# A state-space layer written out, its modulation columns read in place, and a residual of all items formed by GpSimd ahead of it

## The reference

```python
# layer 0: attention, then a stack of six local-attention and feed-forward blocks
x = x + ga * attn0(layernorm(x) * (1 + ca) + sa)
x = x + gb * ffn0(layernorm(x) * (1 + cb) + sb)      # this sum is "x3" below
# layer 1, with its own six vectors
h = layernorm(x) * (1 + ca) + sa
x = x + ga * state_space(h)                          # this sum is "x4"
h = layernorm(x) * (1 + cb) + sb
x = x + gb * (h @ (W + lilora).T + b)                # this sum is "x5", the output
```

## Time and profile before

| | |
|---|---|
| median of 3 runs | 4745.26 us (4742.04 to 4746.15) |
| the profiled execution | 4740.36 us |
| its span in the trace | 4738.6 us |
| granted TensorE clock, mean | 0.957 |
| `phase_c` | from about 4015.8 us to the end |
| from the first scan of item 6 to that of item 7 | 40.97 us |

### The profile page before, as it was taken

The page is one execution under the profiler, slowest core; times in us unless marked ns, Lnnn a source line. Parts: engine busy times, 40 slices in busy tenths (PEclk is TensorE's granted clock), DMA queues, the critical chain, the costliest instruction groups (busy, mean ns, idle before and its releaser), DMA issues. The chain is left out here.

```text
span 4738.6 us, 123474 instructions
## 1 busy us (share of the span) xinstructions
PE 4256.0 (90%) x45166; PEld 3182.7 (67%) x45166; DVE 4026.9 (85%) x7275; ACT 3756.6 (79%) x11543; POOL 3543.5 (75%) x2504
## 2 busy tenths in 40 slices
PE   6998699999999999999999999999999997688887
PEld 3555477777777777777777777777777775445453
DVE  4776798989989989889889899899998895598887
ACT  2555588888888888888888888888888886777774
POOL 0010699999999889999999999999899994444544
PEclk9999799999999999999999999999999998788888
DMA  1000111112111111111111112111111111000000
GB/s 26 7 6 2 47 51 38 45 42 55 52 40 45 45 52 51 40 44 45 52 47 44 43 47 54 45 44 41 49 51 41 45 39 31 0 4 3 3 3 5
DMA packets 118563, 168.62 MB, mean 36 GB/s; under 512 B 26563, under 2 KB 44422, under 8 KB 118022
## 3 DMA queue, kind: packets, MB, share of 16 engines
q1 hardware_dynamic: 109246, 160.92, 12.8%
q10 hardware_dynamic: 8776, 0.45, 0.1%
HBM read 20.79 MB, written 2.10 MB: 5 GB/s over the span
## 5 line engine op out<-in xcount | busy, mean ns | idle before, releaser
L1371 POOL TENSOR_TENSOR b_w<-b_w,b_vt 128x512 f32<-128x512 f32 x768 | 1174.5, 1539 | 256.1 <-DVE b_vt L1285 158.5
L1375 POOL TENSOR_TENSOR b_rn<-b_ssm,all_neg_half 128x16 f32<-128x16 f32 x384 | 1177.4, 3066 | 32.0
L1182 ACT ACTIVATE b_Pr<-ps,b_nm 128x96 f32<-128x96 f32 x3072 | 1000.5, 353 | 0.6
L1182 ACT ACTIVATION_READ_ACCUMULATOR b_Pr<-ps,b_nm 128x1 f32 x3072 | 677.1, 220 | 0.0
L1225 ACT ACTIVATE b_PT<-ps 96x512 f32<-96x512 f32 x768 | 456.3, 594 | 234.8 <-PE ps L1035 222.0
L1334 DVE TENSOR_TENSOR b_Pr<-b_Pr,b_rinv 128x384 f32<-128x384 f32 x768 | 614.2, 800 | 26.3
L1069 PE MATMUL ps<-b_Whi,b_xlo 128*128 128x512 f32 x1152 | 585.4, 508 | 32.9 <-DVE b_vt L1285 18.1
L998 PE MATMUL ps<-all_ident,b_w 128*128 128x128 f32 x3072 | 478.5, 288 | 141.5 <-ACT b_qkT L1153 99.9
L1283 DVE TENSOR_TENSOR b_w<-ps,until_b_rotab 128x512 f32<-128x512 f32 x768 | 523.7, 682 | 60.3 <-ACT b_sq L1202 57.3
L1153 ACT ACTIVATE b_qkT<-ps 128x512 f32<-128x512 f32 x768 | 460.6, 612 | 84.7 <-PE ps L998 83.4
L1285 DVE TENSOR_TENSOR b_vt<-ps,until_b_rotab 128x512 f32<-128x512 f32 x768 | 521.8, 679 | 0.0
(11 more groups left out here) (256 smaller groups left out, 9348.6 us busy)
## 6 DMA issues: line engine op xcount, KB each, us to landing
b_V<-b_Vraw SPq DMA_DIRECT2D x384, 192.0 KB, 2.6
b_V<-b_Vraw SPq DMA_DIRECT2D x384, 128.0 KB, 2.4
b_V<-b_Vraw SPq DMA_DIRECT2D x192, 64.0 KB, 2.2
b_Wraw<-in_L_ffn_Wqkv SPq DMA_DIRECT2D x36, 256.0 KB, 3.3
b_Wo<-in_L_ffn_Wo SPq DMA_DIRECT2D x6, 512.0 KB, 4.1
a_xtok<-in_L_attn_hidden_states SPq DMA_DIRECT2D x16, 128.0 KB, 2.1
out<-c_xout SPq DMA_DIRECT2D x16, 128.0 KB, 1.8
b_W<-in_L_ffn_W SPq DMA_DIRECT2D x6, 341.0 KB, 3.6
```

What stands on the lines that cost most here:

```text
L1182: last = nc.scalar.activation(s.Pr[:, r % 2, j, i], ps[:, S_BANK[j], i * KEYS:(i + 1) * KEYS], ACT.Exp, bias=s.nm[:, r, j, i:i + 1], accum ...
L1371: nc.gpsimd.tensor_tensor(rows, rows, s.vt[:, i % 4], ALU.add).then_inc(s.pool_add, 1)
L1375: nc.gpsimd.tensor_tensor(s.rn[:, j], s.ssm[:, j], g.neg_half[:, 0:HB], ALU.pow).then_inc(s.pool_r, 1)
```

## The change

`phase_c` is written out in full: no loop, so every item number is a constant. With constants the modulation columns are read in place from `all_mod`, and the three small tiles, their copies and the semaphores for them go. x3 is no longer made item by item on DVE and copied back by POOL. POOL makes it for all 16 items ahead of its first step, in place in `all_xT`: a multiplication by the gate (a column broadcast over 256), a wait, and an addition of `all_x2T`. PE transposes item m from `all_xT` as soon as that item is ready, and DVE waits once for all 16 before the first x4.

```diff
-DVE_X3, DVE_XD, DVE_Y, DVE_STATS1, DVE_X4, DVE_DELTA, DVE_STATS2, DVE_X5 = 3, 3, 5, 6, 7, 5, 8, 13
+DVE_XD, DVE_Y, DVE_STATS1, DVE_X4, DVE_DELTA, DVE_STATS2, DVE_X5 = 3, 5, 6, 7, 5, 8, 13
-POOL_X3, POOL_STATS1, POOL_STATS2 = 12, 1, 12
+POOL_STATS1, POOL_STATS2 = 1, 12
 def phase_c_steps(engine, body):
-    def whole(n):
+    for n in range(-2, NB + 2):
         body(StepC(n, n % 2, *[0 <= n + d < NB for d in (2, 1, 0, -1, -2)]))
-    for n in range(-2, 2):
-        whole(n)
-    with engine.Fori(1, NB // 2 - 1) as pair:
-        for odd in range(2):
-            body(StepC(2 * pair + odd, odd, True, True, True, True, True))
-    for n in range(NB - 2, NB + 2):
-        whole(n)
...
 # DVE
-                if step.inner:
-                    m_seq, m_at = known(m), known(m * NT)
                 if step.tail:
-                    t_at, gate = known(t * NT), known(t & 3)
-                    wait(dve, s.x5_ready, t)
-                    copy_mod(s.md_tail, 1, known(t), 2, 6).then_inc(s.md_tail_ready, 1)
+                    gates, x_tail = g.mod[:, 1, t], g.xT[:, t * NT:(t + 1) * NT]
...
                     if step.tail and slot == DVE_X4:
+                        if t == 0:
+                            dve.wait_ge(s.x3_ready, NB)
                         dve.wait_ge(s.op_full, t + 1)
...
-                    if step.inner and slot == DVE_X3:
-                        wait(dve, s.hT_ready, m)
-                        copy_mod(s.md_inner, 1, m_seq, 0, 2)
-                        copy_mod(s.md_x3, 0, m_seq, 5, 6).then_inc(s.md_ready, 1)
-                        wait(dve, s.x3_kept, m)
-                        dve.wait_ge(s.md_ready, m + 1)
-                        nc.vector.scalar_tensor_tensor(out=s.x3T[:], in0=g.xT[:, bass.ds(m_at, NT)], scalar=s.md_x3[:], in1=g.x2T[:, bass.ds(m_at, NT)],
-                                                       op0=ALU.mult, op1=ALU.add).then_inc(s.x3_ready, 1)
...
 # POOL
-                    if step.inner and slot == POOL_X3:
-                        pool.wait_ge(s.x3_ready, m + 1)
-                        nc.gpsimd.tensor_copy(g.xT[:, bass.ds(m_at, NT)], s.x3T[:]).then_inc(s.x3_kept, 1)
...
+            for m in range(NB):
+                x_item, gate = g.xT[:, m * NT:(m + 1) * NT], g.mod[:, 0, m, 5:6].broadcast_to((P, NT))
+                nc.gpsimd.tensor_tensor(x_item, x_item, gate, ALU.mult).then_inc(s.x3_scaled, 1)
+                pool.wait_ge(s.x3_scaled, m + 1)
+                nc.gpsimd.tensor_tensor(x_item, x_item, g.x2T[:, m * NT:(m + 1) * NT], ALU.add).then_inc(s.x3_ready, 1)
             phase_c_steps(pool, body)
...
 # ACT (hT2 the same with columns 3 and 4 of item t, and without its wait for md_tail_ready)
-                        act.wait_ge(s.md_ready, m + 1)
                         act.wait_ge(s.h_full, m + 1)
-                        nc.scalar.activation(s.hT[:], ps[:, F_BANK, NT:2 * NT], ACT.Identity, bias=s.md_inner[:, 0:1], scale=s.md_inner[:, 1:2]).then_inc(s.hT_ready, 1)
+                        nc.scalar.activation(s.hT[:], ps[:, F_BANK, NT:2 * NT], ACT.Identity, bias=g.mod[:, 1, m, 0:1], scale=g.mod[:, 1, m, 1:2]).then_inc(s.hT_ready, 1)
...
 # PE
-                        transpose_tokens(F_BANK, by_tile(s.x3T)).then_inc(s.x3_full, 1)
+                        transpose_tokens(F_BANK, by_tile(g.xT[:, m * NT:(m + 1) * NT])).then_inc(s.x3_full, 1)
```

More of the change, by code:

```diff
@@ L1436, in phase_c @@
         s.conv_diag = s.sb("conv_diag", [P, CC, TAPS, P]); s.D_diag = s.sb("D_diag", [P, CC, P])
-        s.md_x3 = s.sb("md_x3", [P, 1]); s.md_inner = s.sb("md_inner", [P, 2]); s.md_tail = s.sb("md_tail", [P, 4])
-        s.x3T = s.sb("x3T", [P, NT]); s.x3tok = s.sb("x3tok", [P, TT, P]); s.hT = s.sb("hT", [P, NT]); s.hT2 = s.sb("hT2", [P, NT])
+        s.x3tok = s.sb("x3tok", [P, TT, P]); s.hT = s.sb("hT", [P, NT]); s.hT2 = s.sb("hT2", [P, NT])
         s.xp = s.sb("xp", [P, CC, TAPS - 1 + NT]); s.h = s.sb("h", [P, 2, CC, NT]); s.sr = s.sb("sr", [P, 4, CC, NT])
@@ L1444, in phase_c @@
         s.l1 = LayerNormC(s, "l1"); s.l2 = LayerNormC(s, "l2")
-        s.w_in, s.zeroed, s.built, s.md_ready, s.x3_ready, s.x3_kept, s.x3_full, s.x3tok_ready, s.h_full, s.hT_ready = s.sems(
-            "w_in zeroed built md_ready x3_ready x3_kept x3_full x3tok_ready h_full hT_ready")
+        s.w_in, s.zeroed, s.built, s.x3_scaled, s.x3_ready, s.x3_full, s.x3tok_ready, s.h_full, s.hT_ready = s.sems(
+            "w_in zeroed built x3_scaled x3_ready x3_full x3tok_ready h_full hT_ready")
         s.in_full, s.xp_ready, s.conv_full, s.gate_ready, s.h_ready, s.xd_full, s.rounded, s.xd_ready, s.dl_full = s.sems(
@@ L1452, in phase_c @@
             "bu_dve yc_dve pool_mult rows_ready scan_done y_full y_ready op_full")
-        s.md_tail_ready, s.x4_ready, s.x4_full, s.x4tok_ready, s.h2_full, s.hT2_ready, s.lin_full, s.tmp_ready, s.x5_ready = s.sems(
-            "md_tail_ready x4_ready x4_full x4tok_ready h2_full hT2_ready lin_full tmp_ready x5_ready")
+        s.x4_ready, s.x4_full, s.x4tok_ready, s.h2_full, s.hT2_ready, s.lin_full, s.tmp_ready, s.x5_ready = s.sems(
+            "x4_ready x4_full x4tok_ready h2_full hT2_ready lin_full tmp_ready x5_ready")
         s.out_full, s.xout_ready, s.stored = s.sems("out_full xout_ready stored")
@@ L1531, in body @@
                         nc.vector.tensor_tensor(s.y[:], ps[:, Y_BANK].rearrange("p (c t) -> p c t", c=CC),
[L1532 removed]
+                                                s.sr[:, t % 4], ALU.mult).then_inc(s.y_ready, 1)
                     if step.tail and slot == DVE_X4:
+                        if t == 0:
+                            dve.wait_ge(s.x3_ready, NB)
                         dve.wait_ge(s.op_full, t + 1)
[L1535 removed]
+                        nc.vector.scalar_tensor_tensor(out=s.x4T[:], in0=ps[:, TAIL_BANK, 0:NT], scalar=gates[:, 2:3], in1=x_tail,
                                                        op0=ALU.mult, op1=ALU.add).then_inc(s.x4_ready, 1)
[L1537 to L1544 removed]
                     if step.tail and slot == DVE_STATS2:
@@ L1549, in body @@
                         dve.wait_ge(s.tmp_ready, t + 1)
-                        nc.vector.scalar_tensor_tensor(out=s.x5T[:], in0=s.tmp[:], scalar=s.md_tail[:, 3:4], in1=s.x4T[:], op0=ALU.mult, op1=ALU.add).then_inc(s.x5_ready, 1)
+                        nc.vector.scalar_tensor_tensor(out=s.x5T[:], in0=s.tmp[:], scalar=gates[:, 5:6], in1=s.x4T[:], op0=ALU.mult, op1=ALU.add).then_inc(s.x5_ready, 1)
                     if step.delta and slot == DVE_XD:
@@ L1581, in body @@
                 own = step.odd
-                if step.inner:
-                    m_at = m * NT if isinstance(m, int) else pool.snap(m * NT)
                 for slot in range(SLOTS):
@@ L1614, in body @@
                 own, other = step.odd, 1 - step.odd
-                if step.inner:
-                    gate = m & 3 if isinstance(m, int) else act.snap(m & 3)
                 for slot in range(SLOTS):
@@ L1672, in body @@
                         last.then_inc(s.h_ready, 1)
-                        nc.scalar.activation(s.sr[:, bass.ds(gate, 1)].rearrange("p a c t -> p (a c) t"), ps[:, F_BANK].rearrange("p (c t) -> p c t", c=CC),
+                        nc.scalar.activation(s.sr[:, m % 4], ps[:, F_BANK].rearrange("p (c t) -> p c t", c=CC),
                                              ACT.Silu).then_inc(s.gate_ready, 1)
@@ L1681, in body @@
                     if step.tail and slot == ACT_HT2:
-                        act.wait_ge(s.md_tail_ready, t + 1)
                         act.wait_ge(s.h2_full, t + 1)
-                        nc.scalar.activation(s.hT2[:], ps[:, TAIL_BANK, 0:NT], ACT.Identity, bias=s.md_tail[:, 1:2], scale=s.md_tail[:, 2:3]).then_inc(s.hT2_ready, 1)
+                        nc.scalar.activation(s.hT2[:], ps[:, TAIL_BANK, 0:NT], ACT.Identity, bias=g.mod[:, 1, t, 3:4], scale=g.mod[:, 1, t, 4:5]).then_inc(s.hT2_ready, 1)
             phase_c_steps(act, body)
```

4 lines of the change are left out of this document (removed).

## The result

The changed kernel takes 4757.89 us (median of 7 runs, 4753.08 to 4765.60), the kernel before 4742.08 us in the runs beside it (7 runs, 4738.03 to 4746.15). The ratio is 1.0034, with a 95% interval of 1.0025 to 1.0044: slower by 16 us. Forecast were 4762.7 us within 4752 to 4770, and slower by 17.4 us. Of the 4.8 us between 4762.7 and 4757.9, 3.2 are the base: the forecast started from a median of 3 runs, 4745.26, which 7 runs put at 4742.08.

The account below looks back on a forecast made before the run. Bound by a circle from DVE's scan and y through PE, ScalarE and POOL; the prologue delays the first LayerNorm. +19.2 - 1.1 - 0.7 = +17.4 us on 4745.26 gives 4762.7, range 4752 to 4770.

Parts of the forecast that it names:

- sign of being wrong: Layer's begin: the forecast fails if the first scan shifts by much less than POOL's first LayerNorm, forecast 19.2 us late.
- The price of an item: POOL's prologue: multiplication, wait and addition for one item's x3 cost 1.36 us, 21.8 us for 16 items.
- The hold by DVE: POOL's prologue: DVE's ten diagonal operations and selector hold POOL for their whole time, 6.4 us added to the delay.
- The first rival, no hold: POOL's prologue: DVE does not hold POOL, so +11 us, or +9.4 with full loop gain; 4755 to 4756, chance 0.14.
- DVE's 1.83 us per step: Each step: removed column copies and x3 update free this DVE time, worth nothing because DVE then waits 2.1 us for POOL.
- the rival with DVE in the circle: Loop steps: DVE's 1.83 us and POOL's 0.19 shorten each of 14 steps; net -9.8 us, 4735.5, chance 0.07.
- The circle of hand-overs: Each step: scan and y on DVE, then PE, a ScalarE copy, POOL, scan; sets the period of 40.97 us.
- step 14: Kernel before, no item to prepare: DVE waits 2.16 us for POOL instead of 0.30; period 41.00 us, not shorter.
- The gains in the loop: Layer's steps: POOL's shorter products give -1.1 us over 14 steps, and step 1's tiny LayerNorm operation -0.7 us.
- The loop's turns and written-out code: Two rivals: six loop turns cost time, net +6.6, 4752, chance 0.06; written-out code is slower, +6, 4769, chance 0.08.

Follow-up runs that it names:

- e1: Changed kernel with only item 0's x3 formed ahead of POOL's first LayerNorm, items 1 to 15 right behind it; 4740.2 us, 0.9998 of the kernel before.
- e2: Changed kernel with x3 of items 0 to 7 formed ahead of the first LayerNorm, 8 to 15 behind it; 4744.9 us, 1.0006 of the kernel before.
- e4: Kernel before, loop and copied columns kept, with POOL making all x3 ahead of its steps and ScalarE copying each item's for PE; 4757.9 us, ratio 1.0031.
- e7: Changed kernel with POOL waiting for DVE's selector before it begins forming x3; 4765.6 us in one run.
- e3: Changed kernel, written out with columns in place, but x3 made per item on DVE and copied back by POOL; 4742.3 us, 1.0000 of the kernel before.
- e9: e1 plus 7 superfluous PE multiplications per step in PE's idle gap; 4744.2 us, 1.0008 of the kernel before.
- e12: e1 plus 10 superfluous PE multiplications per step, 8 in PE's gap and 2 ahead of the out-projection; 1.0076 of the kernel before.
- e5: e1 with product B3 moved from POOL to DVE, so ScalarE no longer copies its row; 4736.7 us, 0.9990 of the kernel before.
- e8: Kernel before plus 7 superfluous PE multiplications per step in PE's idle gap of 3.6 us; 4743.6 us, ratio 1.0009.
- e6: Kernel before, DVE still making x3, with product B3 moved from POOL to DVE; 4747.8 us in its one run.

## Why the prediction was right, and where its terms were off

*The place and the sign.* Right, and shown by e1, e2 and e4: the loss follows the number of items ahead of the first LayerNorm (16: 17.1 us late, 8: 6.1, 1: 0.1), and it is the same with the loop kept. The forecast named as a sign of being wrong that the first scan shifts by much less than the LayerNorm; it shifts by 14.5 of 17.1 us, and in e2 by 3.3 of 6.1, for a reason that was not in the sum (below).

*The price of an item.* 1.36 us forecast, 1.37 measured (0.61 + 0.07 + 0.72, with the overlap).

*The hold by DVE.* 6.4 us forecast, 4.4 measured: 4.20 by the selector and 3 x 0.06 by the small operations. Adding the ten small operations whole, at 0.20 each, was the mistake: they held POOL for 0.2 us in all and waited themselves (0.59 us in the row above instead of 0.28), so the selector ended 9.2 us after the begin instead of 6.4 (forecast: 13 to 15), hidden as forecast. The prediction's argument from the selector's two SBUF inputs covers its 4.41 us, not the 2.0 of the diagonals, which read one matrix and one column each. The delay was 17.1 us instead of 19.2. The first rival, no hold, is refuted by e7.

*DVE's 1.83 us per step are worth nothing.* Right for the change; e1 shows it (0.9998), and the rival with DVE in the circle fell. But the reason given was too narrow. The wait for POOL did take their place (2.22 us instead of 0.30). The circle of hand-overs as written, though, would have passed on 0.2 us to each period in e3 and e4, and it didn't. So step 14, which the prediction read as proof of the wait, has a period of 41.00 us that the same holder may explain as well.

*The gains in the loop.* -1.1 us for POOL's shorter products and -0.7 for step 1 were forecast; the rest of the layer came out at 664.1 against 664.0, so both are 0. POOL's products did get shorter (4.95 us), and the tiny operation of step 1 took 0.19 us again instead of 4.42; step 1 still took 41.40 us.

*The loop's turns and written-out code.* Neither rival: e3 and e1 are both equal to the kernel before. In six of the nine written-out kernels (the changed one, e1, e2, e7, e9, e12) one step does lose time: from step 8 to 9 the period is 41.22 to 41.33 us where the loop has 40.96 (44.41 after 43.74 in e12), and POOL's last product ends 0.48 us ahead of the scan instead of 0.13. In the changed kernel the next periods are 40.79, 40.88, 40.92 and 40.94, so 0.3 of the 0.36 us is made up again. Its cause is open. The Trainium skill ("Runtime: NRT & Kernel Launch", Instruction fetch mechanics) warns of taken branches; no run here shows a cost of the six turns: the rest is 664.0 us with the loop in e4 and without it in e1.

*What was not in the sum.* From the LayerNorm to the first scan the kernel before takes 49.6 us and the changed one 47.0. Of these 2.6 us, 2.3 lie in the first convolution, timeline of PE before and after:

```profile
4033.17 5.98 PE L1782 MATMUL ps<-c_xp,c_conv_diag 128*128 128x256 f32 x16 [0.69 <-ACT c_xp L1677]
```

```profile
4054.53 3.72 PE L1753 MATMUL ps<-c_xp,c_conv_diag 128*128 128x256 f32 x16 [0.69 <-ACT c_xp L1649]
```

The granted clock came up ahead of it in the changed kernel and during it in the kernel before. The other profiles bear on whether that is chance. In nine of the ten executions without a long prologue the clock comes up 22 us after the layer's begin, the convolution starts at 17.4 and takes 5.93 to 6.12 us; the tenth is e3, where the clock comes up at 15.4 and it takes 3.72. In the four with a delay it starts at 23.1 (e2), 34.2 (changed, e4) and 36.6 us (e7), with the clock up, and takes 3.72 or 3.73. So the delay itself most likely gives these 2.3 us back, by moving the convolution behind the rise of the clock; e3 shows that the rise can also come early without it, for a reason that no run shows.

*How the errors add up.* The profiled layers differ by 17.1 - 2.6 + 0.1 = 14.6 us, the medians of the runs by 15.8. The forecast had 19.2 - 1.1 - 0.7 = 17.4. Its hold was 2.1 us too large and it lacked the 2.6, while the 1.8 us of gains in the loop that it subtracted did not come: part of the closeness is errors that cancel.

## What to carry to other kernels

Work that is put ahead of an engine's first step delays in full whatever serial work is queued behind it, even if all of it is off the busiest engine; ask which operation of the old order is first on that engine, and let only what it needs go ahead of it (e1 takes the whole loss back by moving 15 of 16 items behind one LayerNorm). Freeing an engine that then waits gains nothing by itself, but it can make a second move pay: B3 on DVE gains 3.5 us after it and costs some 6 us without it (one run). And where many variants end at the same period, test that period with a step that must shorten it at once, and read the first steps apart from the late ones.

## What the runs showed of the hardware that was not expected

- The period of a step settles at 40.94 to 40.98 us in the kernel before, the changed one, e1 to e5, e7 and e8, though the part from PE's spread to the scan is anything from 5.52 us (e5) to 6.61 (e3). The fall of PE's clock comes every 40.96 us in them from the second step at the latest, and the scans close up to it: in e5 from 39.82, in the kernel before from 41.42. A single longer step in the changed kernel (41.33) is followed by shorter ones (40.79, 40.88). That the clock holds the period is supported by this, but e9 (40.87) and e6 (41.18) don't keep to it, and no version kept the clock up for a whole step, so it isn't settled.
- A GpSimd addition of 0.72 us took 4.92 us beside a VectorE operation of 4.41 us with two inputs in SBUF; beside VectorE's operations of 0.28 us with one such matrix it took 0.78, and those took up to 0.74.
- Filling PE's idle time by superfluous matrix multiplications moved the slow stretch of the clock (from 9 to 12 and then to 26 us after the scan) and never gained time: 1.0009 with 7, 1.0073 with 10.
- In written-out steps a wait ended about 0.1 us later than in the loop: from POOL's last product to the scan 0.13 us in e3 and 0.03 in e4. The kernel before has both: 0.03 in its loop, 0.13 in its written-out steps 1 and 14.
